# Last attention: the query features of each quarter's second pair of tiles made on Pool

## The reference

```python
center = jnp.tanh(ao[..., :P]) * PI
weights = jnp.exp(-0.5 * deltas ** 2 / (width ** 2 + 1e-06))
off_ph = center[:, :, :, None, :] + deltas[..., None] * 0.1
oc, os_ = (jnp.cos(off_ph), jnp.sin(off_ph))
qc = (pce * oc - pse * os_).reshape(B, L, H * Wn, P)
qs = (pse * oc + pce * os_).reshape(B, L, H * Wn, P)
retrieved = (jnp.einsum('blpd,blhp->blhd', mem1_cos, qc) + jnp.einsum('blpd,blhp->blhd', mem1_sin, qs)) / sqrtP
ws = (retrieved * weights[..., None]).sum(axis=3)
head_out = ws / (weights.sum(axis=3, keepdims=True) + 1e-06)
```

## Time and profile before

| what | us |
|---|---|
| median of 3 runs (range) | 1288.37 (1287.47 to 1289.93) |
| profiled execution | 1287.64 |
| its span in the trace | 1285.9 |
| PE busy in the span | 1184.1 (92%) |
| DVE busy | 768.2 (60%) |
| ACT busy | 639.7 (50%) |
| POOL busy | 523.1 (41%) |
| stretch 973 to 1020 (first quarter): PE / DVE / POOL busy | 35.64 / 40.46 / 27.75 of 47 |
| stretch 1020 to 1070 (second quarter): PE / DVE / POOL busy | 42.84 / 47.11 / 9.03 of 50 |
| stretch 1070 to 1121 (third quarter): PE / DVE / POOL busy | 45.01 / 42.83 / 11.52 of 51 |
| stretch 1121 to 1190 (fourth quarter and behind): PE / DVE / POOL busy | 55.91 / 52.71 / 16.73 of 69 |

### The profile page before, as it was taken

The page is one execution under the profiler, slowest core; times in us unless marked ns, Lnnn a source line. Parts: engine busy times, 40 slices in busy tenths (PEclk is TensorE's granted clock), DMA queues, the critical chain, the costliest instruction groups (busy, mean ns, idle before and its releaser), DMA issues.

```text
span 1285.9 us, 27645 instructions
## 1 busy us (share of the span) xinstructions
PE 1184.1 (92%) x10479; PEld 765.3 (60%) x10479; DVE 768.2 (60%) x1651; ACT 639.7 (50%) x1453; POOL 523.1 (41%) x1114
## 2 busy tenths in 40 slices
PE   7999999999999999999999999499865798878897
PEld 6665665666666666666666666354443576766443
DVE  5565555655556656566565564225359898896553
ACT  1336556556555554554554555124037766844554
POOL 3111444754545545644555545231876212412100
PEclk9989999999999999999999999799986786868999
DMA  4100000000000000000000000111111000000001
GB/s 88 18 5 2 2 2 2 4 6 2 4 2 2 3 2 3 2 2 2 3 2 2 3 2 3 33 66 68 19 17 11 3 1 1 10 8 2 13 13 24
DMA packets 34753, 14.69 MB, mean 11 GB/s; under 512 B 31412, under 2 KB 32020, under 8 KB 34623
## 3 DMA queue, kind: packets, MB, share of 16 engines
q1 hardware_dynamic: 30015, 11.02, 3.8%
q0 software_dynamic: 4608, 1.91, 1.6%
HBM read 6.53 MB, written 7.27 MB: 11 GB/s over the span
## 4 chain that ended last, share of the span: by engine, by line
PE 73%; DVE 12%; POOL 5%; issue 5%; ACT 3%; DMA 1%; SPq 0%; POOLq 0%; DVEq 0%; ACTq 0%
PE psum L765 21%; PE psum L746 10%; PE psum L671 9%; PE psum L737 8%; PE psum L721 4%; POOL XN L1356 3%; PE psum L656 2%; DVE arena L2071 2%; PE psum L1013 1%; PE psum L1061 1%; PE psum L1037 1%; PE psum L564 1%; PE psum L577 1%; PE psum L821 1%; PE psum L834 1%
## 5 line engine op out<-in xcount | busy, mean ns | idle before, releaser
L1487 ACT ACTIVATE arena<-psum 125x500 f32<-125x500 f32 x576 | 306.9, 585 | 329.6 <-PE psum L746 329.6
L1873 DVE TENSOR_REDUCE arena<-psum 125x1 f32<-125x500 f32 x384 | 242.6, 674 | 184.6 <-PE psum L671 184.5
L671 PE MATMUL psum<-arena 32*125 32x500 f32 (+1 forms) x1536 | 321.9, 515 | 0.3 <-DVE arena L1860 0.3
L765 PE MATMUL psum<-arena,XN 125*64 125x250 f32 x2304 | 307.1, 387 | 0.2 <-ACT arena L1487 0.2
L746 PE MATMUL psum<-arena 32*125 32x250 f32 x2304 | 290.0, 368 | 0.0
L746 PEld LDWEIGHTS psum<-arena 32*125 32x125 f32 x2304 | 213.6, 182 | 11.2 <-issue 0.5
L765 PEld LDWEIGHTS psum<-arena,XN 125*64 125x64 f32 x2304 | 140.0, 136 | 120.8 <-issue 78.0
L1876 DVE TENSOR_REDUCE arena<-psum 125x2 f32<-125x500 f32 x192 | 121.4, 674 | 68.9 <-PE psum L671 64.8
L671 PEld LDWEIGHTS psum<-arena 32*125 32x125 f32 x1536 | 127.0, 182 | 3.5 <-issue 1.0
L737 PE MATMUL psum<-arena,onesb 3*125 3x500 bf16 x576 | 122.2, 421 | 0.0
L1279 POOL TENSOR_SCALAR arena<-arena 125x4 bf16<-125x4 f32 x96 | 22.2, 231 | 192.7 <-DVE arena L1881 191.0
(11 more groups left out here) (369 smaller groups left out, 1873.6 us busy)
## 6 DMA issues: line engine op xcount, KB each, us to landing
arena<-arena SPq DMA_DIRECT2D x192, 1.5 KB
expert_in<-XN SPq DMA_DIRECT2D x8, 256.0 KB, 4.8
arena<-expert_in SPq DMA_DIRECT2D x4, 512.0 KB, 5.2
expert_out<-arena SPq DMA_DIRECT2D x4, 512.0 KB, 2.6
out<-H SPq DMA_DIRECT2D x16, 93.8 KB
expert_in<-XN,slot_in POOLq DMA_INDIRECT x48
XN<-expert_out,slot_out POOLq DMA_INDIRECT x48
arena<-in_L_ffn_w SPq DMA_DIRECT2D x2, 256.0 KB
```

Of the source, the lines that this page charges most:

```text
L671: last = pe.matmul(ps[0:R, at_:at_ + hi - lo], QH[row:row + 32, b, g, j * R:(j + 1) * R], KH[row:row + 32, b, g, lo:hi], start=True, stop= ...
L765: last = pe.matmul(ctx_bank[64 * h2:64 * h2 + 64, 0:THIRD], XN[:, p, c, a, :], PR[:, x % 4, h2, i * THIRD:(i + 1) * THIRD], start=(c == 0) ...
L1487: act.activation(PR[:, x % 4, h2, :], st_bank[(2 * x + h2) % 3][0:R, 0:2 * THIRD], ACT.Exp)\
L1873: dve.reduce_max(MX[:, q % 2, 0, 2 * h2 + tile:2 * h2 + tile + 1], ps[0:R, 0:2 * THIRD], AX)\
```

## The change

The chunks 1, 4, 7 and 10, the second pair of tiles of each quarter, are made on Pool instead of DVE (`on_pool`). The arithmetic is the same, but it is done in two parts, one tile each, of 11 instructions (the sums of the two batches stay together), with scratch of its own in `qkp` and `vox`, tiles that the earlier attention has left. PE's `features` of those tiles waits for that tile's part (qf_pool) instead of for the pair. ACT's `memory_features` of such a chunk waits for the products of its second part (prod_pool) and stands one tile later in ACT's order: after `hidden` of the next quarter, ahead of the tile copies of the second tile. The last gather (`gather(3)`) now follows chunk 1 on Pool.

```diff
+        PT2 = qkp[0:R].rearrange("r a b c -> r (a b c)").rearrange("r (i n p) -> r i n p", i=4, p=PP)
+        spare = vox[0:R].rearrange("r a b -> r (a b)")
+        UV2 = spare[:, 0:128].rearrange("r (i g p) -> r i g p", i=2, p=PP)
+        UT2 = spare[:, 128:384].rearrange("r (i g p) -> r i g p", i=4, p=PP)
...
+        def on_pool(q):
+
+            return q % 3 in ((1,) if q >= 3 else (1,))
+
+        def chunk_at(q, own, pools, part=1):
+
+            k = len([n for n in range(q) if on_pool(n) == on_pool(q)])
+            return (S[pools], 2 * k + part + 1) if on_pool(q) else (S[own], k + 1)
+
...
-                pe.wait_ge(S["qf_ready"], x // 2 + 1)
+                pe.wait_ge(*chunk_at(x // 2, "qf_ready", "qf_pool", x % 2))
...
+            def chunk(q):
+
+                p, c = divmod(q, 3)
+                g = slice(2 * NJ * (p % 3) + 4 * c, 2 * NJ * (p % 3) + 4 * c + 4)
+                pool.wait_ge(S["cosines"], 2 * (p + 1))
+                pool.wait_ge(S["wab"], p + 1)
+                for part in range(2):
+                    g0 = g.start + 2 * part
+                    cs = CS[:, :, 4 * g0:4 * g0 + 8, :]
+                    for i in range(2):
+                        w = WA[:, i:i + 2, 16 * q + 8 * part:16 * q + 8 * part + 8].unsqueeze(3)\
+                            .to_broadcast([R, 2, 8, PP])
+                        last = pool.tensor_tensor(PT2[:, 2 * i:2 * i + 2], cs, w, ALU.mult)
+                    last.then_inc(S["prod_pool"], 1)
+                    pool.wait_ge(*chunk_at(q, "prod", "prod_pool", part))
+                    pool.tensor_tensor(PT2[:, 0], PT2[:, 0], PT2[:, 1], ALU.subtract)
+                    link(pool.tensor_tensor(PT2[:, 2], PT2[:, 2], PT2[:, 3], ALU.add))
+                    h4 = PT2.rearrange("r (n i) (g h) p -> r n i g (h p)", i=2, g=2)[:, :, 0]
+                    link(pool.tensor_tensor(h4[:, :, :, 0:64], h4[:, :, :, 0:64], h4[:, :, :, 64:128], ALU.add))
+                    link(pool.tensor_tensor(UV2, h4[:, :, :, 0:32], h4[:, :, :, 32:64], ALU.add))
+                    j = 2 * c + part
+                    cp, sp_ = (trig[:, i, j * PP:(j + 1) * PP].unsqueeze(1).to_broadcast([R, 2, PP]) for i in (0, 1))
+                    pool.tensor_tensor(UT2[:, 0], UV2[:, 0], cp, ALU.mult)
+                    pool.tensor_tensor(UT2[:, 1], UV2[:, 1], sp_, ALU.mult)
+                    pool.tensor_tensor(UT2[:, 2], UV2[:, 0], sp_, ALU.mult)
+                    link(pool.tensor_tensor(UT2[:, 3], UV2[:, 1], cp, ALU.mult))
+                    pool.tensor_tensor(QQ[:, g0:g0 + 2, 0:32], UT2[:, 0], UT2[:, 1], ALU.subtract)
+                    link(pool.tensor_tensor(QQ[:, g0:g0 + 2, 32:64], UT2[:, 2], UT2[:, 3], ALU.add))
+                    pool.sem_inc(S["qf_pool"], 1)
+
...
-                    if x == 0:
+                elif kind == "chunk" and on_pool(x):
+                    chunk(x)
+                    if x == 1:
                         gather(3)
...
-                act.wait_ge(S["prod"], q + 1)
+                act.wait_ge(*chunk_at(q, "prod", "prod_pool"))
...
-                elif kind == "chunk":
+                elif kind == "chunk" and not on_pool(x):
                     memory_features(x)
                 elif kind == "features":
+                    if x % NJ in (1, 3) and on_pool(x // NJ * 3 + x % NJ // 2 + 1):
+                        memory_features(x // NJ * 3 + x % NJ // 2 + 1)
                     feature_tiles(x)
...
-                dve.wait_ge(S["prod"], q + 1)
+                dve.wait_ge(*chunk_at(q, "prod", "prod_pool"))
...
-                elif kind == "chunk":
+                elif kind == "chunk" and not on_pool(x):
                     chunk(x)
```

More of the change, by code:

```diff
@@ L261, in build @@
             "att_h", "rc_ready", "lnb_sum", "lnb_x", "lnb_ssq", "lnb_done", "onehot_sum", "pos_ready", "memory", "big_set", "dma_prep")
-        sem("gate_tanh", "token_bias", "late_zero", "b2_laid", "w_late", "big", "route_ld", "route_ex", "onehot", "slots", "scattered", "xb_loaded0", "xb_loaded1", "xb_loaded2", "xb_loaded3",
+        sem("gate_tanh", "token_bias", "late_zero", "prod_pool", "qf_pool", "b2_laid", "w_late", "big", "route_ld", "route_ex", "onehot", "slots", "scattered", "xb_loaded0", "xb_loaded1", "xb_loaded2", "xb_loaded3",
             "y_stored", "gathered0", "gathered1", "gathered2", "gathered3",
```

## The result

The changed kernel takes 1297.93 us (median of 5 runs, 1295.33 to 1303.02), the kernel before in the same comparison 1288.37 (1286.13 to 1292.02): ratio 1.0076, 95% interval 1.0058 to 1.0094, which is 9.8 us slower (the two medians lie 9.6 apart). A second comparison gave 1.0074 (1.0049 to 1.0100). The profiled execution is the fastest of the five, 1295.33 us with a span of 1293.3; that is 7.7 us (7.4 of span) above the profiled one of before, so a ledger of the two traces has 7.4 us to explain; the other 2.4 lie in executions without a trace. Lines have moved: a chunk of DVE is L2118 to L2136 (before L2071 to L2089), the hidden layer's input L2047 (L2000), the masking L2148 (L2101), PE's first step of the features L923 (L910), its transposes L645 (L632), the two instructions of Pool's layer norm L1261 and L1262 (L1248, L1249), Pool's chunk L1397 to L1412.

The account below looks back on a forecast made before the run. PE was taken to set the pace, waiting for each quarter's first chunk on DVE. Terms 4.2 + 3.8 + 4.0 + 0.9 - 0.3 - 0.3 = +12.3 on 1287.64 gave 1299.9, with 0.7 for the median 1300.6 us; range 1288 to 1307.

Parts of the forecast that it names:

- DVE's relief is worth nothing: Taking the four chunks off DVE gains almost nothing, since DVE would then wait for PE: -0.3 us.
- Turns of whole instructions: DVE and Pool instructions reading SBUF exclude each other for a whole instruction; 1296 to 1304 us, chance 0.56.
- First quarter +3.8: Chunk 0 on DVE meets Pool's chunk 1 from 976.0; seven or eight DVE instructions wait, PE is late by 3.8 us.
- It fits by 0.7 us: Pool's layer-norm scaling, behind the later gather, ends at 1018.2; PE transposes it at 1018.9, so no loss.
- the third rival: Pool late: a part takes 9 us, not 7, PE loses 3.3 once: 1304; chance 0.12 together with long turns.
- Second quarter +4.2: DVE's chunk 3 and Pool's chunk 4 start together; DVE's waits of 3.5 and 0.7 delay PE by 4.2 us.
- Third quarter +4.0: DVE's chunk 6 meets Pool's chunk 7 from 1071.5, both DVE products started or due: 4.0 us.
- Fourth quarter +0.9: Chunk 9 meets nothing; Pool's chunk 10 delays DVE's centring and the start of chunk 11 by 0.9 us.
- Half of the short instructions wait: Of the six short DVE instructions in the second quarter's first chunk, only half wait for Pool: 0.7 us.
- What hides behind DVE's room: DVE's mean and residual meet Pool's second part, about 3 us of waits, hidden by 6.25 us that chunk 4 left free.
- no hindrance: First rival: the engines don't hinder each other, so no change: 1287.3 us; chance 0.13 for 1286 to 1291.
- long turns: Fourth rival: Pool keeps its turn over independent pairs, each long wait doubles: 1308 to 1312; chance 0.12 together with Pool late.

Follow-up runs that it names:

- e1: The kernel before, with most of the work of chunks 1, 4, 7 and 10 left out on DVE and done nowhere; ratio to before 0.9992 (0.9975 to 1.0010).
- e5: The changed kernel, with six of the twelve gather transfers behind chunk 1 moved behind the layer norm's scaling on Pool; ratio to before 1.0092 (1.0069 to 1.0114).
- e7: The changed kernel, with chunk 1 back on DVE and the gather at its old place, chunks 4, 7 and 10 on Pool; 1299.08 us, ratio to before 1.0069.
- e4: The changed kernel, chunk 1 back on DVE, gather at its old place; Pool starts 4 and 7 only after DVE's chunk before them; ratio to before 1.0016.
- e3_extra_memset: The kernel before, with 15 memsets added on Pool at chunks 4 and 7, which write SBUF and read nothing; 1287.12 us, ratio to before 0.9984.
- e8_first_only: The changed kernel, with only chunk 1 on Pool, ahead of the gather, and chunks 4, 7 and 10 back on DVE; 1295.74 us, ratio to before 1.0050.
- a2_after_again: The changed kernel, unchanged, run again beside later runs on the same chip; ratio to before 1.0074 (1.0049 to 1.0100).

## Why the prediction was right, step by step

The forecast was 1300.6 us in a range from 1288 to 1307; the median is 1297.93. The mechanism is the forecast one. The size is 9.8 us of 12.3, and of the profiled pair 7.4 of 12.3. Not all terms were right, and the first quarter's comes out near its measured value by luck, as two errors cancel there.

- **DVE's relief is worth nothing** (-0.3): right. All four chunks left out give 1.0 us, with zero inside the interval (e1).
- **Turns of whole instructions, because both engines read**: right, and shown by what Pool does: memsets cost nothing, long instructions more than short ones of the same total, copies as well.
- **First quarter +3.8**: chunk 0 lasts 9.4 instead of 6.3 us, +3.1. I let four long instructions wait, but at 976.0 only three of them (L2075, L2077, L2078) were still to come; they waited for 2.0 us in all, and the short ones for 1.1. The quarter still lost 4.2 (3.4 in the second trace), because of the next point.
- **"It fits by 0.7 us"**: the step that failed. On Pool's side the times look right to 0.3 us (L1262 done at 1018.47, forecast 1018.2), but chunk 0 began 0.8 us earlier in this trace than in the one that I read (972.55, 973.38). Counted from chunk 0's start Pool was done after 45.9 us, forecast 44.8: 1.1 late, with a gather that began 2.4 us later than I had put it (994.41) and took 20.1 us in place of 22. The larger part is PE's side. I took PE to come 3.8 us later than before throughout, and it came to its end at 1012.46 (1018.61 less 6.15), 39.9 us after chunk 0 began, against 38.5 before (1011.89, by the wait of 3.23 at 1015.12 in the earlier trace rows). PE had made good all but 1.4 us of its delay; 1.2 us of it because the clock was low for 3.4 us behind its restart and not for 5.8. So its wait was 2.9 us longer than before, the third rival in small, and 1.4 + 2.9 make the quarter's 4.2 to 0.1. In the second trace the clock gave nothing back (low for 5.9 us), PE came 2.7 us late and its wait for Pool was 4.1, 0.8 longer than before. By e5 removing the wait for Pool brings 0.7 to 1.5 us in that quarter, and nothing in sum.
- **Second quarter +4.2**: mis-sized; it measured +0.7. Both chunks were to start together; they didn't, as Pool began at 1021.02 and DVE, held up through the first quarter, at 1023.25. Two of Pool's long instructions were out of the way and chunk 3 grew by 1.9 us. Where both do start together, it grows by 3.1 to 3.4 (e5, e7). Another 1.0 us came back through the clock: low for 8.5 us behind the restart at 1031.56 and for 10.5 behind the one at 1026.31. No term of the sum allowed for the order in which the two engines reach a later quarter.
- **Third quarter +4.0**: chunk 6 grew by 3.2; the quarter by 2.6, and by 4.0 in the second trace of the same kernel, where the low clock lasted 10.4 us instead of 7.4.
- **Fourth quarter +0.9**: +0.4 and +0.7 up to chunk 11 in the two traces, and chunk 11 itself, which the ledger leaves out, lasts 6.8 and 6.7 us instead of 6.3. Chunk 9 met nothing, as forecast.
- **Half of the short instructions wait**: about right. In chunk 0 the six take 2.5 us where they take 1.4 undisturbed, in chunk 3 1.7; the long ones of chunk 0 gave 0.85, 0.73 and 0.41.
- **L1248/L1249 no longer fall on DVE's widths** (-0.3): ACT's wait of 0.65 us is gone in the kernel after, where its L1630 follows its table load at 1010.79 at once. No run shows what that is worth in time.
- **What hides behind DVE's room**: right in the change (mean at 1031.43, 2.56 us instead of 1.71, DVE then waits for PE all the same). I had not priced the routing; it is free in the change, and costs 1.4 us once Pool's start is shifted (e4).

The rivals "no hindrance" (1287.3) and "long turns" (1308 to 1312) are both off by more than the interval. No version of the change that was tried beats the kernel before, and e1 shows that none of this kind can by more than about 3 us.

## What to carry to other kernels

Before moving work from DVE to Pool, look at who waits for DVE: if DVE itself would next wait for PE, the move can win nothing, however long the moved chunk is and though it stands on the chain of waits. Then look at what DVE does while Pool works. A DVE instruction with its operands in SBUF can wait for the rest of one reading instruction of Pool, so the price is a count of meetings times the length of *Pool's* instructions; in these traces Pool's memsets and DVE's masking out of PSUM cost nothing, and instructions of 0.3 us on Pool little. And don't carry a delay through the program unchanged: delays of 3.1, 1.9 and 3.2 us in the first chunks came out as quarters 4.2, 0.7 and 2.6 us longer, and as 3.4, 1.0 and 4.0 in another execution of the same kernel (there the chunks grew by 3.1, 2.6 and 3.2).

## What the runs showed of the hardware

**The masking, which takes one operand from PSUM and one from SBUF, is never held up.** All 48 of them in the kernel after (ns min/median/max), with Pool at work beside many:

```profile
L2148 DVE TENSOR_TENSOR arena<-psum,triu x48: 400/408/420, 994.3 to 1176.7; 125x250 f32<-125x250 f32 x48
```

The same line before spans 402 to 420 ns. By these rows a chunk on Pool laid beside the masking alone would not have delayed it. **TENSOR_SCALAR is held up too**, though it reads one tensor: 1.29 us for 0.56 in e4, where Pool's two products of 512 elements run from 1042.93 to 1045.71. The Trainium skill has both ("SBUF — State Buffer", "Who interferes with whom": at most one input in SBUF doesn't contend, unless the instruction runs in a mode that uses both ports, which tensor_scalar can).

**The clock's return varies, and not only by chance.** PE restarts in each quarter after a long wait at 1.2 GHz. Windows of the second quarter (columns as above) in the kernel before, from the restart at 1026.31:

```profile
1026.31:1033.31 7.00, 7.00 (x28) 4.94 (x28) 6.90 (x7) 1.99 (x8) 0.00 (x0) 0.50 0.01 2
1033.31:1036.81 3.50, 3.50 (x7) 1.66 (x6) 3.36 (x10) 3.03 (x10) 0.00 (x0) 0.50 0.00 0
1036.81:1040.31 3.50, 3.50 (x15) 1.67 (x15) 3.47 (x8) 2.20 (x6) 0.00 (x0) 1.00 0.00 0
```

and in e1_left_out, from the restart at 1028.81:

```profile
1028.81:1035.91 7.10, 7.10 (x28) 4.94 (x28) 6.24 (x10) 4.14 (x16) 0.00 (x0) 0.50 0.01 3
1035.91:1039.41 3.50, 3.50 (x11) 1.55 (x10) 1.00 (x2) 2.83 (x5) 0.00 (x0) 1.00 0.00 0
```

PE does the same without a gap in both, and the clock is back after 10.5 us in one and 7.1 in the other. At half speed each us of it is worth half a us, so this quarter can be 1.7 us off with the same work in it: e1's second quarter of 48.4 us is such a case. Over the second to fourth quarters of the fourteen traces it took 7.1 to 10.5 us, in the first quarter 3.4 to 6.3. That is not all scatter of executions. The second to fourth quarters of three kernels in which DVE and PE run alike there agree within 0.4 us. They are 10.5, 8.0 and 8.3 us in the kernel before, 10.2, 7.7 and 8.0 in both e3_extra_memset and e8_first_only. Those of a2_after_again, e5_gather_split and e7_three have 7.3 to 7.6 in the second, 10.2 to 10.4 in the third and 9.0 to 9.9 in the fourth. But the first trace of the kernel after has 8.5, 7.4 and 8.5, unlike its second. So part of it goes with what the program does and part with the execution; what decides it these runs don't show, and a ledger of two traces is no finer than 1 to 2 us a quarter.
